# Queries of a cross-attention layer: key products of two heads over 64 partitions each, weights split piece by piece on ScalarE and VectorE

## The chip, the cores and the metric

The kernel runs on one core of a Trainium2 chip. The metric is the device time of one execution in microseconds (us), taken as the median of several runs.

## What is computed

A Perceiver block in three parts, each added to its input: cross-attention from 16 x 64 tokens of width 256 to a context of 16 x 1601 rows, self-attention, and a mixture of experts with two experts chosen for each token. The change touches only the first steps of the cross-attention. With x normalised over its rows (h), 16 heads of 64:

```
q   = h @ Wq                          # 1024 tokens x 1024, 64 columns a head
k   = ctx @ Wk                        # ctx: normalised context, gain g, bias b
sim = (q . k) * 64 ** -0.5            # for each head
```

The kernel never makes k. It takes the key weights to the query's side: for each head it computes q (64 numbers a token) times that head's 64 x 256 key weights, with the gain folded in and each row of the weights centred. The result, 256 numbers a token and a head, is called the query here, and its product with the plain context rows gives the scores. All products are made to fp32 accuracy from three passes: each operand is split into a high part (rounded to fp32r) and a low part (what is left), and high x low, low x high and high x high are added up in PSUM.

## The kernel before

The program is a row of blocks with a barrier between them: `constants`, `queries`, `attend` (the cross-attention over the context, most of the time), `project_out`, `self_attention`, `route`, `experts`. Each engine runs its own list of instructions in the order written, and semaphores order them across engines. There is no planner: the order in `queries` is written out by hand.

`queries` works on 8 pairs of heads (`p`) and two halves of the 1024 tokens (`th`, 512 each), in this order.

- **Normalising x.** VectorE makes the moments (L83 to L88), POOL the inverse roots (L96), VectorE eight row tiles (L91), TensorE turns them into PSUM banks 0 to 3 (L104), ScalarE copies them to `hT` (L112), VectorE splits that copy into `hTh` (L119) and `hTl` (L121).
- **Weights.** The query weights `wq` come in one transfer of 1 MB. ScalarE makes the high part of all of them in one instruction (L348), POOL the low part in one (L290). The key weights `wk` are scaled, summed and centred by VectorE over all pairs at once (L375 to L382). Their parts `wkh` and `wkl` have a place for each head of a pair, [128, 8, 2, 256]: the 64 partitions of the other head hold zeros, which POOL sets (L287, L292), so that a product over all 128 partitions gives one head's result. ScalarE fills the high parts (L354), POOL the low part of one head and VectorE that of the other (L257).
- **For each pair.** `project(p)` makes q of the two heads (128 rows) in banks 4 and 5, 12 matmuls (`q_banks<-ln_hTh` and `ln_hTl`). ScalarE copies them to `qf` (L361), VectorE splits that into `qh` (L390) and `ql` (L392). Then come the key products, 8 pieces of 3 matmuls (`q_banks<-qh,wkl` and so on), each piece in one of banks 0 to 3. ScalarE empties every even piece (L368) and VectorE every odd one (L342) into `stage`, and SP sends half a pair, two transfers of 512 KB, to the scratch `QT` in HBM (L280) once both engines have done it. TensorE's order is project(0), project(1), keys(0), project(2), keys(1), and so on.
- **Beside it.** VectorE makes statistics of the first context (L408) after pairs 2 to 4 and normalises it (L416) after pairs 6 and 7, with a root on POOL between.

The block ends when every transfer of `stage` has landed (L283). `attend` begins with loads of the queries from `QT` (L592), so it can't overlap.

Of the kernel before, what the change touches and what calls it, by code (L numbers as in the profile page):

```python
# [18 lines left out]
P = 128  # L19
# [15 lines left out]
EPS = 1e-5  # L35
SCALE = DH ** -0.5
# [14 lines left out]
class LayerNorm:  # L51
# [5 lines left out]
    def __init__(self, nc, sb, ps, sem, tag, x, ident, halfpow, split, xn=None):  # L57
# [6 lines left out]
        self.hT = sb(f"{tag}_hT", [P, DC, TOK], F32)  # L64
# [14 lines left out]
    def vector_normalise(self, v, arrived=None):  # L79
        for i in range(TT):  # L80
# [7 lines left out]
        v.tensor_scalar(self.ve[:, :], self.mv[:, :, 1], EPS, None, ALU.add).then_inc(self.veps, 1)  # L88
        v.wait_ge(self.root, 1)
# [25 lines left out]
    def vector_split(self, v):  # L115
# [97 lines left out]
def queries(nc, res_x, x_in, ident, halfpow, Wq, WkT, QT, ctx_in, turned_in, turned_last, cx, gain, bias, ln_g, ln_b,  # L213
# [6 lines left out]
    with ExitStack() as ctx:  # L220
# [8 lines left out]

        gain_row = sb("gain_row", [P, DIM], F32)  # L230
        wk_sum, wk_mean = sb("wk_sum", [P, PAIRS], F32), sb("wk_mean", [P, PAIRS], F32)
# [9 lines left out]
        row_in, wk_scaled, wk_summed, wk_meaned, wk_centred = (sem("row_in"), sem("wk_scaled"), sem("wk_summed"),  # L241
                                                               sem("wk_meaned"), sem("wk_centred"))
        wk_zero, wk_high, wk_low = sem("wk_zero"), sem("wk_high"), sem("wk_low")
        q_made, q_copied, q_high, q_low = sem("q_made"), sem("q_copied"), sem("q_high"), sem("q_low")
        k_made, k_act, k_dve = sem("k_made"), sem("k_act"), sem("k_dve")
        stored = [sem("stored0"), sem("stored1")]
# [4 lines left out]
        pieces = [(th, hh, c) for th in range(2) for hh in range(2) for c in range(DC)]  # L251
# [1810 lines left out]
```

## Time and profile before

| what | value |
|---|---|
| median of 3 runs | 1900.95 us (1899.97 to 1907.53) |
| the profiled execution's own time | 1907.26 us |
| its span in the trace | 1905.5 us |
| PE, DVE, ACT, POOL busy in the span | 92%, 82%, 66%, 10% |
| end of the query stage in the trace | about 109.7 us |

How to read it: times in the trace are from the span's start. PE is TensorE's matmuls, PEld its weight loads (they overlap PE), DVE VectorE, ACT ScalarE, POOL GpSimd, SPq the queue from which SP issues transfers. A matmul's duration includes the way through the array, so in a dense stretch the distance from start to start is what counts. In a row of stretches the columns are the stretch, its length, busy time and number of instructions of PE, PEld, DVE, ACT and POOL, the granted share of TensorE's full clock (1.00 is 2.4 GHz, 0.50 is 1.2 GHz), the busy share of the DMA engines and GB/s. In a row of the timeline: start, duration (from the first start to the last end if merged), engine, line, operation, output and inputs, count, and in brackets the engine's idle time before it and what ended it. In a group's row: count, then busy time and mean ns of one, then idle time before.

### The profile page before, as it was taken

How to read it: one execution, taken by the hardware profiler on the slowest of the kernel's cores; microseconds unless marked ns; L12 is line 12 of the kernel's file. 1: busy time of each engine (PE TensorE's matmuls, PEld its weight loads, DVE VectorE, ACT ScalarE, POOL GpSimd, SP SyncE). 2: the span in 40 equal slices, each digit the busy share in tenths (PEclk: the TensorE clock that was granted, in tenths of full speed). 3: DMA queues.
4: the chain of work that ended last, by engine and by line, in shares of the span. 5: the costliest groups of instructions: out<-in, count | busy, mean ns of one | idle time of the engine just before them, and what ended most of it. 6: DMA issues, size and time to landing. Idle time of an engine off the chain costs nothing. (4 is left out here: it accounts for less than half of the span.)

```text
span 1905.5 us, 31862 instructions
## 1 busy us (share of the span) xinstructions
PE 1747.0 (92%) x9242; PEld 1446.3 (76%) x9242; DVE 1555.0 (82%) x2956; ACT 1258.5 (66%) x2228; POOL 187.6 (10%) x152
## 2 busy tenths in 40 slices
PE   4969999999999999999999999996878639999994
PEld 3857888888888888888888888873664439999994
DVE  7669989989998998998998999884757557878863
ACT  2438778778778778777787787773534336777751
POOL 4000000000000000000000000001016340000003
PEclk9989999999999999999999999997989869999997
DMA  4642222222213222222222222025630056666632
GB/s 143 260 156 79 88 71 69 84 59 81 85 54 87 73 66 74 78 74 70 76 80 70 73 81 60 12 67 156 189 128 1 1 194 210 213 203 221 217 98 78
DMA packets 170338, 199.02 MB, mean 104 GB/s; under 512 B 19080, under 2 KB 130848, under 8 KB 170272
## 3 DMA queue, kind: packets, MB, share of 16 engines
q1 hardware_dynamic: 168736, 194.00, 32.4%
q0 software_dynamic: 1536, 4.20, 0.7%
q8 instruction: 34, 0.56, 0.1%
q14 instruction: 32, 0.26, 0.0%
HBM read 153.53 MB, written 44.63 MB: 104 GB/s over the span
## 5 line engine op out<-in xcount | busy, mean ns | idle before, releaser
L707 ACT ACTIVATE s<-score,rnow 128x512 f32<-128x512 f32 (+1 forms) x416 | 286.7, 689 | 255.9 <-PE score L129 251.3
L127 PE MATMUL score<-qsh,tl 128*128 128x512 f32 (+1 forms) x832 | 331.6, 399 | 15.9 <-DVE qsl L766 13.6
L128 PE MATMUL score<-qsl,th 128*128 128x512 f32 (+1 forms) x832 | 326.1, 392 | 0.0
L129 PE MATMUL score<-qsh,th 128*128 128x512 f32 (+1 forms) x832 | 325.8, 392 | 0.0
L127 PE MATMUL acc<-ph,cl 128*128 128x512 f32 (+1 forms) x832 | 324.7, 390 | 0.8 <-DVE pl L745 0.7
L128 PE MATMUL acc<-pl,ch 128*128 128x512 f32 (+1 forms) x832 | 324.5, 390 | 0.0
L129 PE MATMUL acc<-ph,ch 128*128 128x512 f32 (+1 forms) x832 | 324.4, 390 | 0.0
L739 DVE TENSOR_TENSOR s<-s,misc 128x512 f32<-128x512 f32 (+1 forms) x416 | 281.8, 677 | 9.1 <-PE misc L670 7.6
L745 DVE TENSOR_TENSOR pl<-s,ph 128x512 fp32r<-128x512 f32 (+1 forms) x416 | 283.8, 682 | 1.6 <-ACT ph L688 1.6
L688 ACT ACTIVATE ph<-s 128x512 fp32r<-128x512 f32 (+1 forms) x416 | 259.1, 623 | 2.3 <-PE acc L129 1.7
L693 ACT ACTIVATE s<-s 128x512 f32<-128x512 f32 (+1 forms) x416 | 258.4, 621 | 2.1 <-DVE s L739 2.1
L757 DVE TENSOR_TENSOR top<-top,s 128x512 f32<-128x512 f32 (+1 forms) x352 | 240.4, 683 | 6.0 <-ACT s L707 5.9
L127 PEld LDWEIGHTS score<-qsh,tl 128*128 128x128 f32 (+1 forms) x832 | 153.6, 185 | 50.4 <-issue 14.0
L127 PEld LDWEIGHTS acc<-ph,cl 128*128 128x128 f32 (+1 forms) x832 | 156.2, 188 | 37.2 <-issue 2.2
L129 PEld LDWEIGHTS score<-qsh,th 128*128 128x128 f32 (+1 forms) x832 | 153.5, 184 | 37.2
L128 PEld LDWEIGHTS acc<-pl,ch 128*128 128x128 f32 (+1 forms) x832 | 156.3, 188 | 33.3
L129 PEld LDWEIGHTS acc<-ph,ch 128*128 128x128 f32 (+1 forms) x832 | 156.2, 188 | 33.0
L128 PEld LDWEIGHTS score<-qsl,th 128*128 128x128 f32 (+1 forms) x832 | 153.8, 185 | 34.3
L208 POOL TENSOR_TENSOR rstd<-ve,halfpow 128x13 f32<-128x13 f32 x16 | 38.9, 2430 | 1036.5 <-DVE ve L204 1036.5
L1849 DVE TENSOR_TENSOR wl<-wr,wh 128x2048 fp32r<-128x2048 f32 (+1 forms) x60 | 120.0, 2019 | 18.7 <-ACT wh L1786 18.7
L127 PE MATMUL pp<-e_zh,wl 128*128 128x256 f32 x480 | 135.1, 281 | 0.0
L128 PE MATMUL pp<-e_zl,wh 128*128 128x256 f32 x480 | 134.0, 279 | 0.0
(265 smaller groups left out, 3183.7 us busy)
## 6 DMA issues: line engine op xcount, KB each, us to landing
raw<-in_ctx_in SPq DMA_DIRECT2D x192, 128.0 KB, 2.1
turned<-in_turned_in SPq DMA_DIRECT2D x48, 512.0 KB, 3.7
wr<-in_W SPq DMA_DIRECT2D x45, 512.0 KB
queries_scratch<-stage SPq DMA_DIRECT2D x32, 512.0 KB, 3.6
qr<-queries_scratch SPq DMA_DIRECT2D x64, 256.0 KB, 3.6
outputs_scratch<-o SPq DMA_DIRECT2D x64, 256.0 KB, 3.0
at<-outputs_scratch SPq DMA_DIRECT2D x16, 1024.0 KB, 6.5
wr<-in_Wg SPq DMA_DIRECT2D x15, 1024.0 KB
```

What stands on the lines that cost most here:

```text
L127: pe.matmul(out, wl, mh, start=first, stop=False, **more)
L128: pe.matmul(out, wh, ml, start=False, stop=False, **more)
L129: return pe.matmul(out, wh, mh, start=False, stop=last, **more)
L208: pool.tensor_tensor(self.rstd[:, :], self.ve[:, :], halfpow[:, 0:KT], ALU.pow).then_inc(c_rstd, 1)
L688: act.activation(ph[0:n, ring(t), :], s[0:n, u, t, :], ACT.Copy).then_inc(p_high, 1)
L693: act.activation(s[0:n, u, t, :], s[0:n, u, t, :], ACT.Exp, scale=SCALE).then_inc(expd, 1)
L707: act.activation(s[0:n, u, t, :], score[0:n, slot(0, u, t) % 2, :], ACT.Copy, scale=rnow[0:n, t:t + 1]).then_inc(copied, 1)
L739: v.tensor_tensor(s[0:n, u, t, :], s[0:n, u, t, :], misc[0:n, u], ALU.subtract).then_inc(shifted, 1)
L745: v.tensor_tensor(pl[0:n, ring(t), :], s[0:n, u, t, :], ph[0:n, ring(t), :].bitcast(F32), ALU.subtract).then_inc(p_low, 1)
L757: v.tensor_tensor(top[0:n, :], top[0:n, :], s[0:n, u, t, :], ALU.max).then_inc(maxed, 1)
L1849: v.tensor_tensor(wl[:, b, parts[n]], wr[:, parts[n]], wh[:, b, parts[n]].bitcast(F32), ALU.subtract).then_inc(w_low[n], 1)
```

## The change

- The zero halves of `wkh` and `wkl` go. They are now [128, 8, 256], and a key product takes the 64 partitions of one head (`head(hh)`) of weights and of q. For each half `th` and chunk `c` (a group `g`, four a pair) six matmuls alternate between the two heads, and each head has its own bank of the group's two. There are three such places ("rooms": banks 0 and 1, 2 and 3, 6 and 7), so TensorE waits for group g - 3 to be emptied.
- ScalarE empties three of the four banks of groups (c=0, both heads; c=1, first head), VectorE the fourth.
- The copies `hT` (here) and `qf` go: ScalarE makes the high part straight from PSUM and VectorE the low part from PSUM and the high part, per bank.
- `wq` comes in four pieces of two pairs each (`CUTS`), `wk` in two. ScalarE splits off the high part of a piece and VectorE the low part. Piece 0 comes before pair 0, and pieces 1 to 3 after the copies of pairs 0, 2 and 4. The key weights are scaled and summed pair by pair on VectorE (`centre`), the mean is taken off inside the splits.
- POOL keeps the roots and one small memset.
- `stage` has three places for a pair instead of two, and SP sends each group of 512 KB as soon as it is complete.

```diff
+    def scalar_high(self, act):
         for th in range(2):
-            cols = slice(th * HALF, (th + 1) * HALF)
-            v.wait_ge(self.copied, 2 * th + 2)
-            v.tensor_copy(self.hTh[:, :, cols], self.hT[:, :, cols]).then_inc(self.high, 1)
-            v.wait_ge(self.high, th + 1)
-            v.tensor_tensor(self.hTl[:, :, cols], self.hT[:, :, cols], self.hTh[:, :, cols].bitcast(F32),
-                            ALU.subtract).then_inc(self.low, 1)
+            for c in range(DC):
+                act.wait_ge(self.turned, 2 * th + c + 1)
+                act.activation(self.hTh[:, c, th * HALF:(th + 1) * HALF], self.ps[:, 2 * th + c, :],
+                               ACT.Copy).then_inc(self.high, 1)
+
+    def vector_low(self, v):
+        for th in range(2):
+            for c in range(DC):
+                cols = slice(th * HALF, (th + 1) * HALF)
+                v.wait_ge(self.high, 2 * th + c + 1)
+                v.tensor_tensor(self.hTl[:, c, cols], self.ps[:, 2 * th + c, :], self.hTh[:, c, cols].bitcast(F32),
+                                ALU.subtract).then_inc(self.low, 1)
...
-        wkh = sb("wkh", [P, PAIRS, 2, DIM], F32R)
-        wkl = sb("wkl", [P, PAIRS, 2, DIM], F32R)
-        qf = sb("qf", [P, 2, TOK], F32)
+        wk_sum, wk_less = sb("wk_sum", [P, PAIRS], F32), sb("wk_less", [P, PAIRS], F32)
+        wkh = sb("wkh", [P, PAIRS, DIM], F32R)
+        wkl = sb("wkl", [P, PAIRS, DIM], F32R)
         qh = sb("qh", [P, 2, TOK], F32R)
         ql = sb("ql", [P, 2, TOK], F32R)
-        stage = sb("stage", [P, 2, 2, DC, B // 2, 2, NQ], F32)
-
-        wq_in, wk_in = sem("wq_in"), sem("wk_in")
+        stage = sb("stage", [P, STAGES, 2, DC, B // 2, 2, NQ], F32)
...
+        def act_taken(g):
+
+            return 3 * (g // 2) + 2 + g % 2
+
+        def dve_taken(g):
+
+            return g // 2 + g % 2
+
+        def room(g):
+
+            return bank[:, (0, 2, 6)[g % 3]:(0, 2, 6)[g % 3] + 2, :]
...
+                def weights(j):
+                    sp.dma_start(wq[:, :, cut(j)], Wq.rearrange("(c p) n -> p c n", p=P)[:, :, cut(j)]
+                                 ).then_inc(wq_in[j], 16)
+
+                keys = WkT.rearrange("(j p) d -> p j d", p=P)
+                weights(0)
+                sp.dma_start(wk[:, 0:2, :], keys[:, 0:2, :]).then_inc(wk_in[0], 16)
                 sp.dma_start(gain_row[:, :], g_row.rearrange("(a d) -> a d", a=1).broadcast_to([P, DIM])
                              ).then_inc(row_in, 16)
+                weights(1)
+                sp.dma_start(wk[:, 2:PAIRS, :], keys[:, 2:PAIRS, :]).then_inc(wk_in[1], 16)
+                for j in range(2, CUTS):
+                    weights(j)
...
-                        sp.wait_ge(k_act, 4 * p + 2 * (th + 1))
-                        sp.wait_ge(k_dve, 4 * p + 2 * (th + 1))
+                            g = 4 * p + 2 * th + c
+                            sp.wait_ge(k_act, act_taken(g))
+                            wait(sp, k_dve, dve_taken(g))
...
-                pool.memset(wkh[:, :, :, :].bitcast(F32), 0.0).then_inc(wk_zero, 1)
-                pool.wait_ge(wq_high, 1)
-                pool.tensor_tensor(wql[:, :, :], wq[:, :, :], wqh[:, :, :].bitcast(F32), ALU.subtract
-                                   ).then_inc(wq_low, 1)
-                pool.memset(wkl[:, :, :, :].bitcast(F32), 0.0).then_inc(wk_zero, 1)
-                pool.wait_ge(wk_zero, 2)
-                low_keys(pool, 0)
...
+                    if p % 2 == 0:
+                        pe.wait_ge(wq_low, p // 2 + 1)
...
-                    for n, (th, hh, c) in enumerate(pieces):
-                        g = len(pieces) * p + n
-                        if g >= 4:
-                            pe.wait_ge(k_act if g % 2 == 0 else k_dve, (g - 4) // 2 + 1)
-                        t = slice(th * HALF, (th + 1) * HALF)
-                        w = slice(c * P, (c + 1) * P)
-                        three_passes(pe, bank[:, g % 4, :], wkh[:, p, hh, w], wkl[:, p, hh, w],
-                                     qh[:, p % 2, t], ql[:, p % 2, t], True, True).then_inc(k_made, 1)
-
-            def take(eng, copy, p, parity, mine):
-
-                for n, (th, hh, c) in enumerate(pieces):
-                    if n % 2 != parity:
-                        continue
-                    g = len(pieces) * p + n
-                    eng.wait_ge(k_made, g + 1)
-                    if p >= 2:
-                        eng.wait_ge(stored[p % 2], 64 * (p // 2))
-                    copy(stage[:, p % 2, th, c, :, hh, :],
-                         bank[:, g % 4, :].rearrange("p (b t) -> p b t", t=NQ)).then_inc(mine, 1)
+                    pe.wait_ge(wk_low, p + 1)
+                    for th in range(2):
+                        pe.wait_ge(q_low, 2 * p + th + 1)
+                        for c in range(DC):
+                            g = 4 * p + 2 * th + c
+                            if g >= 3:
+                                pe.wait_ge(k_act, act_taken(g - 3))
+                                wait(pe, k_dve, dve_taken(g - 3))
+                            t = slice(th * HALF, (th + 1) * HALF)
+                            w = slice(c * P, (c + 1) * P)
+                            for n, (wx, qx) in enumerate(((wkl, qh), (wkh, ql), (wkh, qh))):
+                                for hh in range(2):
+                                    m = pe.matmul(room(g)[:, hh, :], wx[head(hh), p, w], qx[head(hh), p % 2, t],
+                                                  start=n == 0, stop=n == 2)
+                                    if n == 2:
+                                        m.then_inc(k_made, 1)
...
+                def high_weights(j):
+                    act.wait_ge(wq_in[j], 16)
+                    act.activation(wqh[:, :, cut(j)], wq[:, :, cut(j)], ACT.Copy).then_inc(wq_high, 1)
+
+                def high_keys(p):
+                    act.wait_ge(wk_meaned, p + 1)
+                    act.activation(wkh[:, p, :], wk[:, p, :], ACT.Identity, bias=wk_less[:, p:p + 1]
+                                   ).then_inc(wk_high, 1)
+
+                def high_queries(p):
                     for th in range(2):
                         act.wait_ge(q_made, 2 * p + th + 1)
                         if p >= 2:
-                            act.wait_ge(q_low, p - 1)
-                        act.activation(qf[:, p % 2, th * HALF:(th + 1) * HALF], bank[:, 4 + th, :],
-                                       ACT.Copy).then_inc(q_copied, 1)
-
-                copy_q(0)
+                            act.wait_ge(k_made, 2 * (4 * (p - 2) + 4))
+                        act.activation(qh[:, p % 2, th * HALF:(th + 1) * HALF], bank[:, 4 + th, :],
+                                       ACT.Copy).then_inc(q_high, 1)
+
+                high_weights(0)
+                high_keys(0)
+                ln.scalar_high(act)
+                high_queries(0)
                 for p in range(PAIRS):
                     if p + 1 < PAIRS:
-                        copy_q(p + 1)
-                    take(act, lambda o, i: act.activation(o, i, ACT.Copy), p, 0, k_act)
+                        high_queries(p + 1)
+                        high_keys(p + 1)
+                    for th in range(2):
+                        for c, hh in ((0, 0), (0, 1), (1, 0)):
+                            take(act, lambda o, i: act.activation(o, i, ACT.Copy), p, th, c, hh, k_act)
+                    if p % 2 == 0 and p // 2 + 1 < CUTS:
+                        high_weights(p // 2 + 1)
...
+                def centre(p):
+                    v.wait_ge(wk_in[0 if p < 2 else 1], 16)
+                    if p == 0:
+                        v.wait_ge(row_in, 16)
+                    v.tensor_tensor(wk[:, p, :], wk[:, p, :], gain_row[:, :], ALU.mult).then_inc(wk_scaled, 1)
+                    v.wait_ge(wk_scaled, p + 1)
+                    v.tensor_reduce(wk_sum[:, p:p + 1], wk[:, p, :], AX_X, ALU.add).then_inc(wk_summed, 1)
+                    v.wait_ge(wk_summed, p + 1)
+                    v.tensor_scalar(wk_less[:, p:p + 1], wk_sum[:, p:p + 1], -1.0 / DIM, None, ALU.mult
+                                    ).then_inc(wk_meaned, 1)
+
+                def low_keys(p):
+                    v.wait_ge(wk_high, p + 1)
+                    v.scalar_tensor_tensor(out=wkl[:, p, :], in0=wk[:, p, :], scalar=wk_less[:, p:p + 1],
+                                           in1=wkh[:, p, :].bitcast(F32), op0=ALU.add, op1=ALU.subtract
+                                           ).then_inc(wk_low, 1)
+
+                def low_weights(j):
+                    v.wait_ge(wq_high, j + 1)
+                    v.tensor_tensor(wql[:, :, cut(j)], wq[:, :, cut(j)], wqh[:, :, cut(j)].bitcast(F32), ALU.subtract
+                                    ).then_inc(wq_low, 1)
+
+                def low_queries(p):
+                    for th in range(2):
+                        cols = slice(th * HALF, (th + 1) * HALF)
+                        v.wait_ge(q_high, 2 * p + th + 1)
+                        v.tensor_tensor(ql[:, p % 2, cols], bank[:, 4 + th, :], qh[:, p % 2, cols].bitcast(F32),
+                                        ALU.subtract).then_inc(q_low, 1)
+
+                ln.vector_moments(v, x_in)
+                centre(0)
+                ln.vector_rows(v)
+                low_weights(0)
+                ln.vector_low(v)
                 v.wait_ge(wk_meaned, 1)
-                v.tensor_tensor(wk[:, :, :], wk[:, :, :], wk_mean[:, :].unsqueeze(2).broadcast_to([P, PAIRS, DIM]),
-                                ALU.subtract).then_inc(wk_centred, 1)
-                ln.vector_split(v)
-
-                def split_q(p):
-                    v.wait_ge(q_copied, 2 * p + 2)
-                    if p >= 2:
-                        v.wait_ge(k_made, len(pieces) * (p - 1))
-                    v.tensor_copy(qh[:, p % 2, :], qf[:, p % 2, :]).then_inc(q_high, 1)
-                    v.wait_ge(q_high, p + 1)
-                    v.tensor_tensor(ql[:, p % 2, :], qf[:, p % 2, :], qh[:, p % 2, :].bitcast(F32),
-                                    ALU.subtract).then_inc(q_low, 1)
-
-                v.wait_ge(wk_zero, 2)
-                low_keys(v, 1)
-                split_q(0)
+                low_keys(0)
+                low_queries(0)
+                centre(1)
                 for p in range(PAIRS):
                     if p + 1 < PAIRS:
-                        split_q(p + 1)
-                    take(v, v.tensor_copy, p, 1, k_dve)
+                        low_queries(p + 1)
+                        v.wait_ge(wk_meaned, p + 2)
+                        low_keys(p + 1)
+                    for th in range(2):
+                        take(v, v.tensor_copy, p, th, 1, 1, k_dve)
+                        if th == 0 and p + 2 < PAIRS:
+                            centre(p + 2)
+                    if p % 2 == 0 and p // 2 + 1 < CUTS:
+                        low_weights(p // 2 + 1)
```

## Rows read from the trace of the kernel before

**Rows 1.** Busy time by stretch: the query stage's start, its steady part, its end.

```profile
29.30:41.00 11.70, 8.49 (x20) 6.20 (x21) 10.23 (x5) 3.25 (x5) 4.87 (x2) 1.00 0.00 0
41.00:104.00 63.00, 62.67 (x270) 49.63 (x268) 40.84 (x73) 27.46 (x46) 2.67 (x2) 1.00 0.60 240
104.00:122.60 18.60, 5.09 (x12) 4.05 (x13) 8.27 (x20) 3.35 (x10) 0.16 (x2) 0.63 0.75 247
```

**Rows 2.** Timeline, 8 to 36 us, and one row of the last pairs.

```profile
10.05 10.30 DVE L91 TENSOR_SCALAR ln_xn<-res_x,ln_mv,ln_rstd 128x256 f32<-128x256 f32 x8 [1.80 <-POOL ln_rstd L96]
11.72 4.72 POOL L290 TENSOR_TENSOR wql<-wq,wqh 128x2048 fp32r<-128x2048 f32 x1 [1.70 <-ACT wqh L348]
...
29.50 4.77 POOL L257 TENSOR_TENSOR wkl<-wk,wkh 64x2048 fp32r<-64x2048 f32 x1 [9.61 <-ACT wkh L354]
29.91 5.44 DVE L121 TENSOR_TENSOR ln_hTl<-ln_hT,ln_hTh 128x1024 fp32r<-128x1024 f32 x1
35.41 0.79 PE L127 MATMUL q_banks<-ln_hTh,wql 128*128 128x512 f32 x1 [3.09 <-DVE ln_hTl L121]
...
98.56 2.35 DVE L416 TENSOR_SCALAR nrm<-raw,rstd,shift 128x256 f32<-128x256 f32 x7
```

**Rows 3.** Groups of instructions by form, 0 to 160 us.

```profile
L127 PE MATMUL q_banks<-qh,wkl 128*128 128x512 f32 x64 | 25.9, 405 | 0.3 <-DVE stage L342 0.3
L342 DVE COPY stage<-q_banks 128x512 f32<-128x512 f32 x32 | 21.3, 687 | 9.1 <-PE q_banks L129 9.1
L368 ACT ACTIVATE stage<-q_banks 128x512 f32<-128x512 f32 x32 | 19.2, 599 | 21.3 <-PE q_banks L129 20.7
...
L778 DVE TENSOR_TENSOR tl<-turned,th 128x256 fp32r<-128x256 f32 x16 | 6.4, 417 | 5.7 <-ACT th L717 5.7
...
L739 DVE TENSOR_TENSOR s<-s,misc 128x512 f32<-128x512 f32 x6 | 4.1, 680 | 0.0
```

**Rows 4.** Timeline: the first key product of pairs 0 and 1.

```profile
42.11 0.40 PE L127 MATMUL q_banks<-qh,wkl 128*128 128x512 f32 x1
...
50.45 0.39 PE L127 MATMUL q_banks<-qh,wkl 128*128 128x512 f32 x1
```

**Rows 5.** Timeline: the end of the stage and the start of the next.

```profile
103.96 0.69 DVE L342 COPY stage<-q_banks 128x512 f32<-128x512 f32 x1 [0.70 <-PE q_banks L129]
...
104.73 0.83 SPq L280 DMA_DIRECT2D queries_scratch<-stage  x2
109.74 0.83 SPq L178 DMA_DIRECT2D raw<-in_ctx_in  x2
```

**Rows 6.** Transfers from 104 to 110 us: GB/s in 40 slices, and one kind of issue.

```profile
GB/s 328 410 410 410 437 382 437 410 300 410 382 410 382 437 410 410 437 437 410 410 437 355 382 410 437 382 437 328 28 27 27 0 0 0 0 0 0 0 0 0
...
queries_scratch<-stage SPq DMA_DIRECT2D x2, 512.0 KB, 3.8
```

**Rows 7.** Timeline of PE in self-attention: full-width and half-width (64-column) weights.

```profile
1436.05 3.60 PE L1151 MATMUL s_banks<-ln_hT,w_qkv 128*128 128x512 f32 x8
1439.58 2.02 PE L1164 MATMUL s_banks<-w_qkv,ln_hT 128*64 128x128 f32 x32
1441.37 1.94 PE L1179 MATMUL s_banks<-s_kb,s_qT 128*64 128x512 f32 x8
```

**Rows 8.** Timeline of PE in the experts: two matmuls of 256 columns.

```profile
1590.51 0.28 PE L127 MATMUL pp<-e_zh,wl 128*128 128x256 f32 x1
1590.63 0.28 PE L128 MATMUL pp<-e_zl,wh 128*128 128x256 f32 x1
```

**Rows 9.** Busy time by stretch: idle PE and the granted clock behind it.

```profile
1335.10:1338.10 3.00, 0.04 (x1) 0.04 (x1) 2.90 (x1) 2.35 (x3) 2.91 (x1) 0.95 0.24 97
1338.10:1341.50 3.40, 3.40 (x17) 3.40 (x18) 3.40 (x2) 0.00 (x0) 0.00 (x0) 0.54 0.00 0
...
1850.20:1853.50 3.30, 0.04 (x1) 0.00 (x0) 1.60 (x3) 1.47 (x3) 0.00 (x0) 0.95 0.00 0
1853.50:1856.90 3.40, 3.36 (x16) 3.36 (x17) 0.00 (x0) 0.00 (x0) 0.00 (x0) 0.54 0.00 0
...
1358.70:1360.40 1.70, 0.01 (x1) 0.00 (x0) 1.66 (x2) 0.01 (x1) 0.00 (x0) 1.00 0.10 39
1362.00:1365.40 3.40, 3.40 (x12) 2.73 (x12) 2.54 (x2) 1.31 (x2) 0.00 (x0) 0.55 0.84 242
```

More of the change, by code:

```diff
@@ L35 @@
 EPS = 1e-5
+STAGES, CUTS = 3, 4
 SCALE = DH ** -0.5
@@ L63, in __init__ @@
         self.xn = sb(f"{tag}_xn", [P, TT, DIM], F32) if xn is None else xn
-        self.hT = sb(f"{tag}_hT", [P, DC, TOK], F32)
+        if not split:
+            self.hT = sb(f"{tag}_hT", [P, DC, TOK], F32)
         if split:
@@ L79, in vector_normalise, with vector_moments @@
     def vector_normalise(self, v, arrived=None):
+        self.vector_moments(v, arrived)
+        self.vector_rows(v)
+    def vector_moments(self, v, arrived=None):
         for i in range(TT):
@@ L88, in vector_normalise, with vector_rows @@
         v.tensor_scalar(self.ve[:, :], self.mv[:, :, 1], EPS, None, ALU.add).then_inc(self.veps, 1)
+    def vector_rows(self, v):
         v.wait_ge(self.root, 1)
@@ L250, in queries @@
         normed = sem("f_normed")
-        pieces = [(th, hh, c) for th in range(2) for hh in range(2) for c in range(DC)]
-        def low_keys(eng, hh):
-            r = slice(hh * DH, (hh + 1) * DH)
-            eng.wait_ge(wk_high, hh + 1)
-            eng.tensor_tensor(wkl[r, :, hh, :], wk[r, :, :], wkh[r, :, hh, :].bitcast(F32), ALU.subtract
-                              ).then_inc(wk_low, 1)
+        cut = lambda j: slice(j * HEADS * DH // CUTS, (j + 1) * HEADS * DH // CUTS)
+        head = lambda hh: slice(hh * DH, (hh + 1) * DH)
+        def act_taken(g):
[4 more added lines that the diff above has]
+            return bank[:, (0, 2, 6)[g % 3]:(0, 2, 6)[g % 3] + 2, :]
         with nc.Block() as block:
@@ L303, in project @@
                 def project(p):
+                    if p % 2 == 0:
+                        pe.wait_ge(wq_low, p // 2 + 1)
                     for th in range(2):
                         if p >= 1:
-                            pe.wait_ge(q_copied, 2 * (p - 1) + th + 1)
+                            pe.wait_ge(q_low, 2 * (p - 1) + th + 1)
                         else:
-                            pe.wait_ge(ln.low, th + 1)
+                            pe.wait_ge(ln.low, DC * (th + 1))
                         for c in range(DC):
@@ L314, in project @@
                         m.then_inc(q_made, 1)
-                pe.wait_ge(wq_low, 1)
                 project(0)
@@ L345, in _, with take @@
+            def take(eng, copy, p, th, c, hh, mine):
+                g = 4 * p + 2 * th + c
+                eng.wait_ge(k_made, 2 * g + hh + 1)
+                if p >= STAGES:
+                    eng.wait_ge(stored[p % STAGES], 64 * (p // STAGES))
+                copy(stage[:, p % STAGES, th, c, :, hh, :],
+                     room(g)[:, hh, :].rearrange("p (b t) -> p b t", t=NQ)).then_inc(mine, 1)
             @block.scalar
             def _(act):
-                act.wait_ge(wq_in, 16)
@@ L348, in _ @@
-                act.activation(wqh[:, :, :], wq[:, :, :], ACT.Copy).then_inc(wq_high, 1)
-                ln.scalar_copy(act)
-                act.wait_ge(wk_centred, 1)
-                act.wait_ge(wk_zero, 1)
-                for hh in range(2):
-                    r = slice(hh * DH, (hh + 1) * DH)
-                    act.activation(wkh[r, :, hh, :], wk[r, :, :], ACT.Copy).then_inc(wk_high, 1)
-                def copy_q(p):
+                def high_weights(j):
+                    act.wait_ge(wq_in[j], 16)
+                    act.activation(wqh[:, :, cut(j)], wq[:, :, cut(j)], ACT.Copy).then_inc(wq_high, 1)
@@ L370, in _ @@
             @block.vector
             def _(v):
-                ln.vector_normalise(v, x_in)
-                v.wait_ge(wk_in, 16)
-                v.wait_ge(row_in, 16)
-                v.tensor_tensor(wk[:, :, :], wk[:, :, :], gain_row[:, :].unsqueeze(1).broadcast_to([P, PAIRS, DIM]),
-                                ALU.mult).then_inc(wk_scaled, 1)
-                v.wait_ge(wk_scaled, 1)
-                v.tensor_reduce(wk_sum[:, :], wk[:, :, :], AX_X, ALU.add).then_inc(wk_summed, 1)
-                v.wait_ge(wk_summed, 1)
```

28 lines of the change are left out of this document (10 added, 18 removed).

## The prediction

> **What bounds the kernel now.** I read the page first, then busy time by stretch, the timeline of the first 45 us, the groups of the stage, its waits, its transfers, and PE's idle times in the rest of the program. The change touches only `queries`, which ends at 109.7 of 1905.5 us; `attend` starts behind a barrier and loads everything it needs from `QT`, so I take all that follows as unmoved. What counts is how much earlier the last transfer lands.
>
> The stage has three parts. The reader should see first that from 41 to 104 us PE is never idle (62.67 of 63 us, 270 matmuls, 0.232 us each) and DVE and ACT are not full; before that, 20 matmuls take 8.49 us, 0.42 us each, which is the 1.2 GHz level (the clock column has no event there yet and reads 1.00), and after 104 PE stands still [rows 1]. So the middle is bound by PE. The first part is bound by DVE, stretched by POOL: eight row tiles take 10.30 us while POOL is busy with L290 and then a memset, where the like instruction L416 does seven in 2.35 us; later one L121 takes 5.44 us beside L257 on POOL, and PE's second half starts at 35.41 after it [rows 2].
>
> **The change, part by part.**
>
> *Start.* Rows of DVE without POOL beside them: 8 x 2.35/7 = 2.7 instead of 10.3 us [rows 2]. They start at 10.05 as before, since the root precedes them (`centre(0)` fits ahead of it if `gain_row` has landed by some 8.5 us; it now queues behind 1.5 MB instead of 3). Rows end at 12.75. Then the low part of piece 0 of `wq` and four low parts of h, five instructions of the 0.68 us kind (L739, from PSUM [rows 3]), so the first half of h is done at 12.75 + 3 x 0.68 = 14.8, the second at 16.2. ScalarE's high parts (0.60 each) start at 12 and keep ahead. project(0) therefore starts at 14.9, instead of in the mid-thirties for its second half, its 12 matmuls at the low clock take 12 x 0.427 = 5.1 us (to 20.0), project(1) at the high one 12 x 0.227 = 2.7. keys(0) starts at 22.7, against 42.11 [rows 4]: 19.4 us earlier. Here ends the simple part.
>
> *One pair.* Before: 36 matmuls, 50.45 - 42.11 = 8.34 us [rows 4]. After: project is the same 12, 2.7 us. The keys are again 24 matmuls of 512 columns, but each over half the array's rows. If the two heads' matmuls run at once, they take 12 places, 2.7 us; if one after the other, 24 places, 5.45 us. No row of before has such a pair. The nearest have half the columns: eight records with full-width weights take 3.60 us, eight with half-width ones and the same 512 columns 1.94 [rows 7]. So half tiles do get twice the rate in this kernel. A weight load for each is no obstacle at such a rate: loads and matmuls of 256 columns follow each other every 0.12 us [rows 8], and two loads in 0.227 us is that. I take 2.7 us and keep 5.45 as the other end. A change of the tile's shape, twice a pair, costs at most 0.12 us: the eight full-width records are two passes of 512 columns each, 3.41 us at 2.4 GHz, and the half-width ones start 1439.58 - 1436.05 = 3.53 us after the first [rows 7]. I count 0.1 a pair, as one of the two falls into a wait.
>
> What the half-width rows show for columns, the Trainium skill, TensorE: Matmul & The Clock Gate, section Part 3 (packing small matmuls), states for rows: matmuls in different row groups run concurrently. By that page a group costs 0.68 us as in my sum; by the other end, in series, it would be 1.36 us and the time that of rival B. No run here shows it for rows yet.
>
> *ScalarE then sets the pace in places.* Per pair it has two high parts of q, one of the keys (256 columns, some 0.35), six copies: 8 x 0.60 + 0.35 = 5.15 us [rows 3]. With keys(p) starting at 0: group 0 is made at 0.9, but ScalarE is still with the high parts of q and keys for p + 1 until 1.15, copies until 1.15 + 3.6 = 4.75. The room of group 0 is free at 2.35, so group 3 runs 2.45 to 3.1: 0.4 us lost. If the next project may follow, the period is 3.1 + 2.7 + 0.1 = 5.9 us. DVE per pair: two low parts, two copies (0.68 each), key splitting and centring (0.42 kind, four of them, L778), 4.5 us [rows 3], plus 1.8 for five statistics in pairs 2 and 3: hidden, as the next paragraph gives it more time.
>
> *The wait that takes its place.* `project(2)` waits for piece 1 of `wq`, and in the written order ScalarE makes its high part only after all copies of pair 0, VectorE the low part after that. But `project(2)` stands directly behind keys(0) on PE. The same holds for project(4) and project(6). So: copies end at 4.75, high part 5.35, low part 6.05, PE goes on at 6.1 instead of 3.1: idle 3.0 us. Behind it everything waits, PE's keys(1) too, and ScalarE for its next q.
>
> *What the idle time does to the clock.* PE idle for 3.0 and for 3.3 us is followed in both cases by 3.4 us at a granted clock of 0.54, and even 1.7 us idle was soon followed by one at 0.55 [rows 9]. So I count 3.4 us at 1.2 GHz behind each of the three waits: 8 matmuls there, 4 after, 3.4 + 0.9 = 4.3 us for a project instead of 2.7: 1.6 us each. An even pair is then 6.1 + 2.7 + 1.6 = 10.4 us, an odd one 5.9.
>
> *Sum.* keys(6) starts at 22.7 + 3 x (10.4 + 5.9) = 71.6. From there ScalarE has twelve copies in a row: the last ends at 71.6 + 1.15 + 7.2 = 80.0, against 103.96 + 0.69 = 104.65 [rows 5]: 24.7 earlier.
>
> *The transfers' tail.* Before, the last two of 512 KB were issued at 104.73 and the next block began at 109.74 [rows 5]; each landed 3.8 us after its issue, at some 405 GB/s [rows 6], which is 1.3 us for each. In the steady part 2.1 MB in 8.15 us on average is 257 GB/s, far below that. In the last two pairs a group comes every 0.9 us: the first store is issued at 71.6 + 2.4 = 74.0, lands at about 77.7, and seven more at 1.3 us each end at 86.8. Before it was 109.3 or so. The tail gives back 2 us of the 24.7. Net gain: 22.6 us. SP itself issues four transfers a pair, 0.42 us each [rows 5], and `stage` has three places, so neither binds.
>
> Against the profiled execution: 1907.26 - 22.6 = 1884.7 us. That execution lay 6.3 us above the median, so the median should be 1900.95 - 22.6 = **1878 us**.
>
> **Rivals.**
>
> *A. As the sum, but the clock does not fall* (or falls for one wait only). For it: after 1.7 us idle the clock held for another 1.6 us; against: the rows of 3.0 and 3.3 us [rows 9]. Gain 22.6 + 4.8 = 27.4: 1873 to 1874 us.
>
> *B. The two heads' matmuls do not overlap* (the zeros are gone and nothing is won by it). For it: only column tiles are shown [rows 7]. Keys take 5.45 us, the last copy of an even pair ends at 6.3, splits 7.5, project at 7.6 with 2.1 us idle: even 7.6 + 2.7 + 1.6 = 11.9, odd 8.2. keys(6) at 22.7 + 60.3 = 83.0, last copy 11.8 later at 94.8, no queue of transfers: 9.9 earlier, 1891 us; without a fall of the clock 1886.
>
> *C. Slower: each half-array matmul waits for its own weight load.* Place: the six matmuls of a group, where the load of one head's weights can't pass the other's matmul. Price: a load is busy for 49.63/268 = 0.185 us [rows 1], so a matmul would take up to 0.227 + 0.185 = 0.41, a pair's keys 9.9 and the pair 12.6; the splits are hidden then. keys(6) at 22.7 + 75.6 = 98.3, last copy 19.8 + 0.9 later at 119.0: 14 us slower, 1915. It decides from the point where 8 x 24 x t + 6 x 2.7 + 22.7 + 0.9 = 104.65, so t = 0.34 us a matmul. Against: the 0.12 us distance [rows 8] and [rows 7], where loads of a half tile cost nothing.
>
> *D. PE stays at 1.2 GHz for the whole stage*, because it works only half of the time. Project 5.1, keys 5.4; even pairs about 13.1, odd 10.6, keys(6) at 25 + 71 = 96, last copy about 108, 3 us later than before: 1903 to 1904. Against: elsewhere the clock came back after 3.4 us [rows 9], with PE well loaded behind it.
>
> **How the numbers follow.** Forecast (with misjudgements of a few us in the start and the tail) 0.48, A 0.17, B 0.18, C 0.06, D 0.06, something else 0.05 (half of it a partial overlap). What a measurement of this kernel can tell from no change is about 0.5%, 9.5 us, so faster means below 1891.4. The forecast and A are, and B with most of its weight: 0.48 + 0.17 + 0.13 + 0.02 = 0.80. Same: D and the rest of B, 0.13. Slower: 0.07. Range: down to A with the start or the ScalarE chain 5 us shorter (copies back to back at less than their 0.60 us), 1868; up to B's upper end, 1892. That leaves out C, D and the odd rest.
>
> **What would show it.** Row tiles L91 at 0.34 us apart and the first project near 15 us; keys(0) near 23. Two heads' matmuls with nearly the same start, a group of six over 0.68 us. PE idle for about 3 us ahead of project(2), (4) and (6), ended by VectorE's low part of `wq`, with the clock at 0.5 behind it, and no such wait ahead of project(3) and (5). ScalarE copies in a dense row at the end, and transfers at 400 GB/s in the last 10 us; `attend` beginning near 87 us. Wrong it would be if the key matmuls started over 0.3 us apart, if ScalarE waited for `stored`, or if `attend`, once begun, took a different time from before.

## The result and the profile after

| what | before | changed |
|---|---|---|
| median | 1902.95 us (4 runs, 1899.97 to 1907.53) | 1875.07 us (4 runs, 1869.20 to 1877.37) |
| ratio, 95% interval | | 0.9862 [0.9839, 0.9885] |
| profiled execution, its span | 1907.26, 1905.5 us | 1875.03, 1873.3 us |
| start of keys(0) in the trace | 42.11 us | 22.06 us |
| start of the next block in the trace | 109.74 us | 79.15 us |

It was faster by 1.4%; the forecast was 1878 us, with 1868 to 1892 as its range. The median of before is 2.0 us higher here than that of the three runs from which the forecast started. Inside the trace the next block begins 30.6 us earlier, against 22.6 forecast. What follows it is a little different from execution to execution: span less start of the next block is 1795.8 us before, 1794.2 in the changed kernel and 1784.5 to 1796.6 in the variants below. So differences of a few us are read from the start of the next block, not from the whole time.

The start of the stage in the changed kernel's timeline (start, duration, engine, line, operation, count, idle time before), to be held against [rows 2]:

```profile
10.03 0.42 DVE L407 TENSOR_TENSOR wk<-wk,gain_row 128x256 f32<-128x256 f32 x1 [1.90 <-DMA gain_row<-in_g_row]
...
11.01 2.66 DVE L99 TENSOR_SCALAR ln_xn<-res_x,ln_mv,ln_rstd 128x256 f32<-128x256 f32 x8
...
15.62 0.77 PE L141 MATMUL q_banks<-ln_hTh,wql 128*128 128x512 f32 x1
16.18 0.58 PE L142 MATMUL q_banks<-ln_hTl,wqh 128*128 128x512 f32 x1
16.60 0.40 PE L143 MATMUL q_banks<-ln_hTh,wqh 128*128 128x512 f32 x1
```

The eight row tiles take 2.66 us where they took 10.30. Of those 10.30 us a single tile, the seventh of before, had 8.04, from 12.00 to 20.04, while POOL was at its subtraction and then at its memset:

```profile
12.00 8.04 DVE L91 TENSOR_SCALAR ln_xn<-res_x,ln_mv,ln_rstd 128x256 f32<-128x256 f32 x1
```

The tiles start a microsecond late in the changed kernel, because `centre(0)` stands ahead of them and VectorE waits 1.90 us for `gain_row`. The first project starts at 15.62, and from its third matmul on the distance is 0.23 us, that of the full clock.

The pairs, from the same timeline and from busy time by stretch (length, then busy time and count of PE, PEld, DVE, ACT, POOL, granted clock, DMA share, GB/s), against [rows 1, 4]:

```profile
44.58 0.51 PE L354 MATMUL q_banks<-qh,wkl 64*128 64x512 f32 x2
44.91 0.40 PE L354 MATMUL q_banks<-ql,wkh 64*128 64x512 f32 x2
45.15 0.40 PE L354 MATMUL q_banks<-qh,wkh 64*128 64x512 f32 x2
45.38 0.40 PE L354 MATMUL q_banks<-qh,wkl 64*128 64x512 f32 x2
...
55.88 0.50 PE L141 MATMUL q_banks<-ln_hTh,wql 128*128 128x512 f32 x1 [2.23 <-DVE wql L422]
```

Where the tile's shape changes, the distance is longer, here from the keys of pair 1 to project(3):

```profile
33.04 0.39 PE L354 MATMUL q_banks<-qh,wkh 64*128 64x512 f32 x2
33.36 0.50 PE L141 MATMUL q_banks<-ln_hTh,wql 128*128 128x512 f32 x1
33.70 0.40 PE L142 MATMUL q_banks<-ln_hTl,wqh 128*128 128x512 f32 x1
```

By stretch, pair 0 and pair 1:

```profile
22.00:30.30 8.30, 6.07 (x37) 4.26 (x36) 4.60 (x10) 5.05 (x10) 0.00 (x0) 1.00 0.68 265
30.30:36.30 6.00, 6.00 (x37) 4.32 (x36) 3.90 (x9) 4.54 (x9) 0.00 (x0) 1.00 0.53 209
```

The reader should see "x2": the matmuls of the two heads start together, and the next two 0.23 us later. An odd pair takes 6.0 us with PE never idle, an even one 8.3 us with 2.2 us of PE idle, and the clock stays at 1.00 in both. The wait stands where it was forecast: ahead of project(2), (4) and (6), ended by the low part of `wql`, three times in all:

```profile
ACT qh L384 <- PE q_banks L143: 14.7, 13, 2.5
...
PE q_banks L141 <- DVE wql L422: 6.7, 3, 2.2
```

That is the view of who waited for whom, 22 to 80 us (total, times, longest). The end of the stage, against [rows 5]:

```profile
65.80 5.98 ACT L397 ACTIVATE stage<-q_banks 128x512 f32<-128x512 f32 x12
...
70.84 1.28 DVE L365 COPY stage<-q_banks 128x512 f32<-128x512 f32 x2
...
79.15 0.83 SPq L192 DMA_DIRECT2D raw<-in_ctx_in  x2
```

Twelve copies of ScalarE in 5.98 us, 0.49 us apart; the last copy of all ends at 72.1, and 7 us pass until the next block. In these 7 us the transfers run at 380 to 440 GB/s, as in [rows 6]: GB/s of the changed kernel in 40 slices of 58 to 86 us,

```profile
GB/s 380 41 23 29 6 269 404 398 404 404 410 416 293 47 404 416 392 410 415 392 392 427 398 398 410 410 380 439 263 0 0 67 234 225 334 334 205 268 304 287
```

### The profile page after: what moved, and what is told of

Same layout as the page of the kernel before. It is cut to its first block and busy times, and to the rows that moved or that the text cites. A ratio compares the mean times of both kernels' runs of the same rounds, so it can differ in the third digit from the quotient of the medians.

```text
span 1873.3 us, 31942 instructions
## 1 busy us (share of the span) xinstructions
PE 1724.9 (92%) x9242; PEld 1425.8 (76%) x9242; DVE 1530.2 (82%) x2971; ACT 1262.8 (67%) x2253; POOL 172.1 (9%) x148
```

## The experiments

All times of the next block's start are of the profiled execution, to be held against 79.15 us. e3 to e7 were executed once each, so only their stage is read.

**e1_split_before_copies: is the wait due to the written order?**

```diff
                         high_keys(p + 1)
+                    if p % 2 == 0 and p // 2 + 1 < CUTS:
+                        high_weights(p // 2 + 1)
                     for th in range(2):
                         for c, hh in ((0, 0), (0, 1), (1, 0)):
                             take(act, lambda o, i: act.activation(o, i, ACT.Copy), p, th, c, hh, k_act)
-                    if p % 2 == 0 and p // 2 + 1 < CUTS:
-                        high_weights(p // 2 + 1)
```

and the same for `low_weights` on VectorE, between `low_keys` and its copies.

> The query weights' next piece is split before the copies of pairs 0, 2 and 4 instead of behind them, on ScalarE and on VectorE. Theory (the three waits of project(2), (4), (6) are due to the written order alone): no wait of PE for wql, the next block begins 6 to 7 us earlier than 79.15 us, unless transfers hold it: 32 of 1.3 us each from the first at 24.2 can't end before 68. Time about 6 us below the changed kernel. Rival (ScalarE is the bound of a pair anyway, and the wait only shows where its queue ends): the waits move to q_low or to the rooms, under 2 us gained.

The next block began at 73.86 us, 5.3 earlier. The median was 1865.69 us (4 runs, 1863.46 to 1868.77), the ratio to the kernel before 0.9809 [0.9792, 0.9826], which does not meet the changed kernel's interval. The waits for `wql` are gone; in their place PE waits three times 0.31 us for ScalarE:

```profile
24.83 0.50 PE L354 MATMUL q_banks<-qh,wkl 64*128 64x512 f32 x2 [0.31 <-ACT stage L399]
```

The three waits were 6.7 us. An even pair takes 6.47 us now (keys(0) at 22.18, keys(1) at 28.65) instead of 8.27, so 5.4 us are won in three pairs, and keys(0) was 0.1 us later. That is less than the 6 to 7 us expected, since a small part of the wait moved to ScalarE's copies, as the rival had it. In the main the theory holds: the written order makes the waits, and the rival, with less than 2 us, is out. This version has the lowest median of all.

**e2_full_rows: what is the packing worth?**

```diff
-                                    m = pe.matmul(room(g)[:, hh, :], wx[head(hh), p, w], qx[head(hh), p % 2, t],
+                                    m = pe.matmul(room(g)[:, hh, :], wx[:, p, w], qx[:, p % 2, t],
```

> Key products over all 128 partitions instead of a head's own 64 (both heads' weights and q are summed, so the queries are not those of the reference); everything else as in the changed kernel. Theory (the two heads' matmuls run at once in the two halves of the array): the matmuls of a group now start 0.227 us apart one by one, a pair's keys take 5.45 us instead of 2.7, odd pairs 8.2 us instead of 6.0, even ones about 10.1 instead of 8.3, and the next block begins some 14 us later, at about 93 us. Rival (half rows win nothing and the rest of the change made the whole gain): no later than 80 us.

The next block began at 92.18 us, 13.0 later; median 1884.1 us (1882.44 to 1886.03), ratio 0.9900 [0.9884, 0.9917]. The matmuls come one by one now, two of them 0.46 us from the next two:

```profile
32.01 0.62 PE L354 MATMUL q_banks<-qh,wkl 128*128 128x512 f32 x2
32.47 0.63 PE L354 MATMUL q_banks<-ql,wkh 128*128 128x512 f32 x2
```

An odd pair takes 8.22 us (keys(1) at 32.01, keys(2) at 40.23), as expected. The wait for `wql` shrinks to 1.71 us, as the longer products cover some of it. So half-array matmuls do run two at a time, and this is worth 13 of the 30.6 us.

Without a change of shape the 36 matmuls of this pair are 8.22/36 = 0.228 us apart on average; the next matmuls behind the keys start 0.23 us apart at 37.49 and 37.72. In the changed kernel the starts around each change of shape are 0.32 and 0.34 us apart instead of 0.23 twice (33.04, 33.36, 33.70): 0.2 us a change, 0.4 a pair.

**e3_heads_in_turn: do the two heads have to alternate?** The loops over `hh` and over the passes change places.

> Same products, but the three passes of one head and then the three of the other, instead of the heads in alternation. Theory A (a matmul overlaps the one before it only if that is in the other half): per group the third of the first head with the first of the second, and the last with the next group's first, so 4 places of 0.227 us a group instead of 3; about 1 us a pair, partly hidden in the waits of even pairs: next block 4 to 6 us later. Theory B (TensorE picks pairs from its queue): no change. Theory C (each half keeps its own order and runs on by itself): no change in the sum of a group either, but the second head starts with the first.

```profile
44.91 0.51 PE L354 MATMUL q_banks<-qh,wkl 64*128 64x512 f32 x2
45.25 0.41 PE L354 MATMUL q_banks<-ql,wkh 64*128 64x512 f32 x2
45.48 0.41 PE L354 MATMUL q_banks<-qh,wkh 64*128 64x512 f32 x2
```

A group still takes 0.69 us, and the first passes of both heads start together although the second head's is the fourth instruction of the group. So theory A is out, and the rows are as theory C has them: each half of the array goes on by itself. Theory B, in which TensorE picks pairs from its queue, would give the same rows and is not told apart from it. The Trainium skill, TensorE: Matmul & The Clock Gate, section Part 3 (What overlaps and what doesn't), says that matmuls keep the program's order in start and end; these rows show otherwise across the two halves, and the measurement decides.

The next block nevertheless began at 81.09, 1.9 us later. Of these, 0.3 us were there at keys(0) already (22.34). Behind the third wait for `wql`, which had the same 2.2 us, the clock fell:

```profile
54.10:56.20 2.10, 0.00 (x0) 0.00 (x0) 1.51 (x5) 1.37 (x3) 0.00 (x0) 1.00 1.02 398
57.90:61.30 3.40, 3.40 (x11) 2.29 (x11) 0.95 (x4) 1.26 (x3) 2.65 (x2) 0.54 0.38 152
```

The next row is the same span of time in the changed kernel, where it did not: 26 matmuls instead of 11.

```profile
57.80:61.30 3.50, 3.50 (x26) 2.52 (x25) 2.43 (x5) 2.74 (x7) 2.77 (x2) 1.00 0.29 116
```

**e4_pool_subtract and e5_pool_memset: what in POOL's work held VectorE up?** Each adds one instruction behind `ln.pool_root(pool)`:

```diff
+                pool.tensor_tensor(cx.nrm[:, 0:TT, :], res_x[:, :, :], res_x[:, :, :], ALU.subtract).then_inc(st_zero, 1)
```

```diff
+                pool.memset(cx.nrm[:, :, :], 0.0).then_inc(st_zero, 1)
```

> POOL gets one subtraction of 128x2048 from and to SBUF right behind its first root, into a tensor that is overwritten later (it adds work and takes none away). Theory (the row tiles L91 of before were held up by POOL's work): the eight row tiles, 2.66 us in the changed kernel, or the key centring before them, stand still until POOL's 4.7 us are over; keys(0) starts 3 to 4 us later than 22.06, the next block as much. Rival (they were slow because of the loads that landed at the same time, 365 GB/s then): no change, as these loads are still there.

> POOL gets one memset of 128x3328 right behind its first root, an instruction that reads nothing (added work, into a tensor that is overwritten later). At 3.5 us for 4096 elements a partition it takes some 2.9 us, from about 9.9. Theory (any write of POOL to SBUF of this kind holds DVE up, as L91 of before seemed to stand behind the subtraction and the memset alike): the key centring or the row tiles wait until it is over at 12.8, and keys(0) is 2 to 3 us later than 22.06. Rival (only an instruction of POOL that reads SBUF holds DVE up): no change.

With the subtraction keys(0) began at 24.94, 2.9 us later (3 to 4 expected), and with the memset at 24.14, 2.1 us later (2 to 3 expected). So the rival of e4, the loads that landed at the same time, is out. With the subtraction:

```profile
9.88 3.59 POOL L315 TENSOR_TENSOR nrm<-res_x 128x2048 f32<-128x2048 f32 x1
10.00 3.75 DVE L408 TENSOR_TENSOR wk<-wk,gain_row 128x256 f32<-128x256 f32 x1 [1.88 <-DMA gain_row<-in_g_row]
```

With the memset:

```profile
9.98 2.86 POOL L315 MEMSET nrm<- 128x3328 f32 x1
10.80 0.42 DVE L408 TENSOR_TENSOR wk<-wk,gain_row 128x256 f32<-128x256 f32 x1 [2.54 <-DMA gain_row<-in_g_row]
...
11.78 3.57 DVE L99 TENSOR_SCALAR ln_xn<-res_x,ln_mv,ln_rstd 128x256 f32<-128x256 f32 x8
```

and the first of these eight tiles by itself:

```profile
11.78 1.31 DVE L99 TENSOR_SCALAR ln_xn<-res_x,ln_mv,ln_rstd 128x256 f32<-128x256 f32 x1
```

A product of two tensors in SBUF, 0.42 us by itself, took 3.75 beside the subtraction: it ended at 13.75, 0.28 us after POOL's 13.47, so it stood still in between. Beside the memset the same product took its 0.42 us. But the row tiles, one input and scalars, took 3.57 instead of 2.66: the first of them took 1.31 us and ended at 13.09, just behind the memset's end at 12.84, and the other seven came at their usual distance. Another 0.8 us of e5's 2.1 is `gain_row`, which landed later than in the changed kernel. Both theories of e5 were too simple: it depends on both instructions. The Trainium skill, SBUF — State Buffer, section Summary: rules for kernel authors, says that VectorE and GpSimd block each other fully when VectorE is in a two-port mode, or has two SBUF inputs while the GpSimd instruction reads SBUF; the three rows fit that, if the row tiles run in such a mode, which no row shows by itself. The next blocks began at 83.66 and 84.35 us, 4.5 and 5.2 us later. Less the late keys(0), 1.6 and 3.1 us are left, and they are again the clock, which fell behind one wait for `wql` and behind two.

**e6_longer_idle and e7_longer_idle_turned: is it the length of the wait?**

```diff
+                        rows_more = (2, 4, 8)[p // 2]
+                        act.activation(cx.nrm[:, 0:rows_more, :], res_x[:, 0:rows_more, :], ACT.Copy)
                         high_weights(p // 2 + 1)
```

> ScalarE does an extra, unused copy ahead of the late splits of the query weights: 512 elements for the wait of project(2), 1024 for project(4), 2048 for project(6). PE's waits of 2.23 us become about 2.8, 3.2 and 4.1. Theory (the clock falls by where a wait lies in time, and a longer wait meets it more often): at least two of the three are followed by 3.4 us of matmuls 0.43 us apart, each costing 1.6 us; next block 79.15 + 3.4 + 3.2 = 85.8 or later. Rival (2.2 us never lets it fall, and in the two runs where it fell something else did): all three hold, 82.5.

> As e6_longer_idle with the extra copies in the opposite order (2048, 1024, 512): waits of about 4.1, 3.2, 2.8 us. If length decides, the clock falls behind the first two in any case; if the place decides, behind others than in e6_longer_idle.

In e6 the clock held behind 2.75 us, and fell behind 3.17 and 4.03 (next block at 86.24):

```profile
28.50:35.00 6.50, 6.49 (x38) 4.79 (x39) 3.43 (x8) 4.04 (x9) 0.00 (x0) 1.00 0.47 185
40.60:43.70 3.10, 0.00 (x0) 0.00 (x0) 1.53 (x5) 2.32 (x4) 0.00 (x0) 1.00 1.01 406
44.90:48.30 3.40, 3.40 (x11) 2.36 (x9) 1.08 (x3) 0.60 (x1) 0.00 (x0) 0.56 0.19 74
```

In e7 it fell behind all three, 4.02, 3.17 and also 2.75 us (87.85). So of the waits of 2.75 us one of two was followed by a fall, and of the longer ones four of four. Length counts, then: the rival of e6, by which all three hold, is out. Where a wait lies in time may count as well, and these runs do not part the two.

**e8_early_and_rows_last: what bounds the tail?** As e1, and all of `normed` behind the last copies (`if p == 7` with `range(KT)`).

> The splits ahead of the copies as in e1_split_before_copies, and VectorE's first seven normalised context rows (2.34 us between its copies of pairs 6 and 7) go behind its last copy, with the other six. Theory (the tail is bound by the transfers, about 400 GB/s from the first store of pair 6 on): at most 1 us earlier than e1_split_before_copies, whose next block begins at 73.86, since only a short gap of the transfers goes; and the rows, 4.4 us, still end before the last transfer lands. Rival (SP waits for VectorE's late copy of pair 7 and the rest queues behind): 2 us earlier.

The next block began at 73.68, and as keys(0) was 0.17 us earlier too, nothing was won: median 1867.32 us, ratio 0.9816 [0.9795, 0.9836]. VectorE's last copy ended at 66.1 instead of 66.8, and the transfers still took until close to 73.7. The tail is theirs, in this order of the splits.

**e9_before_pool_freed: how much of the start is POOL?** The kernel before with

```diff
                 ln.pool_root(pool)
-                pool.wait_ge(wq_high, 1)
-                pool.tensor_tensor(wql[:, :, :], wq[:, :, :], wqh[:, :, :].bitcast(F32), ALU.subtract
-                                   ).then_inc(wq_low, 1)
+                pool.wait_ge(ln.norm, TT)
                 pool.memset(wkl[:, :, :, :].bitcast(F32), 0.0).then_inc(wk_zero, 1)
-                pool.wait_ge(wk_zero, 2)
-                low_keys(pool, 0)
```

and the subtraction and `low_keys` of the first head on VectorE.

> The kernel before, with POOL's large instructions away from VectorE's start: the low part of the query weights and of the first head's key weights on VectorE, the zeros of wkl on POOL behind the row tiles. Nothing else of the change. Row tiles 10.05 to 12.75; wql 2.3, key weights 6.9, splits of h 3.8: project(0) from about 24.5 with its second half at about 26, keys(0) held by the two low_keys at about 31 to 32, against 42.11. Theory (half of the 20 us at the start is POOL in VectorE's way, half is doing all pairs' weights first): the next block begins about 10 us before 109.74. Rival (it is nearly all POOL, or nearly all the piecewise weights): 17 us or more, or 3 us or less.

```profile
10.42 2.67 DVE L91 TENSOR_SCALAR ln_xn<-res_x,ln_mv,ln_rstd 128x256 f32<-128x256 f32 x8 [1.80 <-POOL ln_rstd L96]
...
32.72 0.47 PE L127 MATMUL q_banks<-qh,wkl 128*128 128x512 f32 x1 [0.89 <-DVE ql L391]
```

keys(0) at 32.72, next block at 100.28, 9.5 us earlier than before; median 1892.57 us, ratio 0.9960 [0.9945, 0.9974]. Of the 20.0 us at the start, 9.4 come from POOL being out of the way, the added work of VectorE taken off, and 10.7 from the rest (weights by pieces, parts from PSUM), which no run divides further. e9 also agrees with e5 on the memset: a product of two tensors takes 2.29 us beside POOL's memset of `wkl`, and the like one behind it, without the memset, takes 2.29 as well.

```profile
13.01 2.29 DVE L370 TENSOR_TENSOR wql<-wq,wqh 128x2048 fp32r<-128x2048 f32 x1
13.15 3.52 POOL L290 MEMSET wkl<- 128x4096 f32 x1 [2.77 <-DVE ln_xn L91]
...
20.06 2.29 DVE L381 TENSOR_TENSOR wk<-wk,wk_mean 128x2048 f32<-128x2048 f32 x1
```

**e10_changed_again**

> The changed kernel itself, to see whether the clock falls behind its three waits of 2.2 us in another execution. It fell behind none of three in its first profile, and behind 4 of the 9 waits of this length in three variants. Theory (where the wait lies in time decides): each wait has some chance of one in three; where it falls, the matmuls are 0.43 us apart for 3.4 us and the next block begins 1.6 us later for each.

Median 1872.08 us (4 runs, 1871.13 to 1874.15), ratio 0.9854 [0.9836, 0.9873]. keys(0) at 22.00, three waits of 2.2 us, and this time the clock fell behind the third; next block at 80.64, 1.5 us later than in the first profile:

```profile
53.70:55.80 2.10, 0.00 (x0) 0.00 (x0) 1.50 (x5) 1.36 (x3) 0.00 (x0) 1.00 1.01 396
57.50:60.90 3.40, 3.40 (x12) 2.22 (x12) 1.09 (x4) 1.42 (x3) 2.65 (x2) 0.52 0.37 147
```

Over all profiles it fell behind 5 of 15 waits of 2.2 us (0 of 3, 1 of 3 in e3, 1 of 3 in e4, 2 of 3 in e5, 1 of 3 in e10), and behind none of the three of 1.71 us in e2. e10 ran on another chip than e1 to e8, and on which the first profile was taken is not on record, so that e10 alone does not show that the chip has no part in it. But e3 to e5, all on one chip, have falls behind some waits of this length and none behind others.

## Why the prediction was right

Most of its mechanism held: PE in the middle and VectorE behind POOL at the start, the two heads at once, a new wait of PE for the next piece of `wq` in three places, and the queue of transfers at the end. One step did not: the clock did not fall behind the three waits. Rival A, in which the clock does not fall or falls for one wait only, had a chance of 0.17, and it is what both profiles of the changed kernel show: a fall behind none of three waits, and behind one of three. The other misses are sizes, nearly all to the side of too slow:

| term | forecast | measured |
|---|---|---|
| keys(0) starts | 22.7 | 22.06 |
| odd pair | 5.9 | 6.0 |
| PE's wait ahead of project(2), (4), (6) | 3.0 | 2.23 |
| loss by the clock behind each | 1.6 | 0 here, about 1.6 where it falls, in 5 of 15 cases |
| even pair | 10.4 | 8.3 |
| keys(6) to the next block | 15.5 | 14.35 |
| next block earlier by | 22.6 | 30.6 |

- *Start.* The gain of 20 us is as worked out, with errors that cancel in part: `gain_row` came at 10.0, not by 8.5, so the first project was 0.7 us late. Only its first two matmuls were slow, where I had counted all 12 at the low clock: project(0) and the short wait behind it took 3.5 us (15.62 to 19.10) instead of 5.1. PE's transposes end just ahead of it now, where 7.7 us of idle time lay before it in the kernel before; that this is the reason is likely but not shown. project(1) took 3.0 us instead of 2.7. e9 shows that the attribution to POOL was right for about half.
- *The pair.* Half rows run two at a time (e2: 13.0 us), so rivals B and C are out: a group takes 0.69 us, forecast 0.68. B's other end, matmuls in series, is what e2 looks like. That the odd pair came out right is in part luck, as two errors cancel. The wait for a room costs hardly 0.1 us and not 0.4, since ScalarE's copies come faster than forecast, and the changes of shape cost 0.4 us a pair and not 0.1.
- *Steady part before.* The forecast took 8.15 us for a pair, but its own rows give 8.34, so 251 GB/s instead of 257. Nothing hangs on it.
- *The wait.* e1 shows its cause. It was 0.77 us shorter than forecast, most of it (0.56) because I took ScalarE's copies at their duration of 0.60 us, but in a dense row they start 0.49 us apart; six take 3.04 us, not 3.6. `[rows 3]` could not show this, as ScalarE was idle ahead of nearly every copy of `stage` before. But the trace of before had it elsewhere, in self-attention, where two copies of the same size out of PSUM start 0.5 us apart:

```profile
1463.94 1.09 ACT L1256 ACTIVATE s_aT<-s_banks 128x512 f32<-128x512 f32 x2
```

- *The clock.* This step failed: 1.6 us behind each of three waits, 4.8 us of the 8.0 in all. The size is right where it happens (1.5 us in e10), but waits of 2.2 us meet it one time in three, and I had rows of 3.0 and 3.3 us, and one of 1.7 that spoke for a fall. With a wait of 3.0 us it would likely have come more often: e6 and e7 have one fall of two at 2.75 us and two of two at 3.17. No execution with waits of 2.2 us shows all three falls of the forecast; e5 shows two.
- *D* is out: PE works 73% of an even pair, and the clock was at 1.00 from 16.7 us on.
- *The tail.* Bound by the transfers, as forecast; e8 shows that copies that end earlier do not help.

Sum of the misses: 0.6 (start) + 3 x 2.1 (even pairs) - 0.3 (odd pairs) + 1.15 (tail) = 7.8 of the 8.0 us. The median fell by 27.9 us and not by 30.6, which is within what the rest of the program varies. So it is luck that the forecast of 1878 us lies only 3 us from the measured 1875: the stage was mis-sized by 8.0 us, and the rest of the program (2.7) and the higher median of before (2.0) hide more than half of that.

The whole 30.6 us divide into 20.0 at the start (about half POOL, half the rest), 13.0 by packing, and a rest of -2.4. The changes of shape are inside the 13.0, as e2 has none. On the minus side of the rest are the three waits (5.3 us by e1) and the longer tail (7.0 us from the last copy to the next block, 5.1 before); on its plus side must be the third room, the smaller transfers and what else the change brings, which no run isolates.

## What to carry to other kernels

When work is cut into pieces so that it starts earlier, ask for each later piece which instruction waits for it and what stands ahead of it in its engine's list: here moving the split of the next piece ahead of the copies, on ScalarE and on VectorE, gave another 5.3 us. Price a dense row of instructions by the distance of starts in a dense stretch, not by the duration of a lone one. And before POOL is given work "beside" VectorE, look whether VectorE's instructions in that stretch grow: 8 row tiles at 10.3 us instead of 2.7, and one of them at 8.04, were the sign.

## What the runs showed of the hardware that I had not expected

- Matmuls over different halves of the rows do not need to alternate in the program: with three of one half and then three of the other, both halves start together (e3, a group of six in 0.69 us either way).
- The same idle time of PE, 2.2 us, is or is not followed by 3.4 us at the low clock, from execution to execution of one program (e10 against the first profile, perhaps on two chips); it costs 1.5 to 1.6 us. What decides it I did not settle; the waits lie in the trace at nearly the same times (they end at 55.88 and 55.84).
- A change between tiles of 128 and of 64 rows costs TensorE about 0.2 us each time (starts 0.32 and 0.34 us apart instead of 0.23 twice); in e2, without such a change, the pair has no such places.
- A memset of POOL lets a product of two SBUF tensors on VectorE run at its 0.42 us (e5) but holds up `tensor_scalar` with one tensor input (the first tile 1.31 us instead of 0.4); a subtraction of POOL holds up the product (3.75 us, e4).
